# An audio tower on one core: the survival test of units A and B moved from VectorE to ScalarE, with new cyclic orders for all engines

## The reference

```python
def _ssm_layer(x, A_log, Dp, W_dbc, W_dt, b_dt):
    A = -jnp.exp(A_log)
    dbc = jnp.einsum('ble,ce->blc', x, W_dbc)
    delta, Bm, Cm = jnp.split(dbc, [DT_RANK, DT_RANK + N_STATE], axis=-1)
    delta = jax.nn.softplus(jnp.einsum('blr,er->ble', delta, W_dt) + b_dt)
    dA = jnp.exp(delta[..., None] * A)
    dBx = (delta * x)[..., None] * Bm[:, :, None, :]
    _, hs = jax.lax.associative_scan(combine, (dA, dBx), axis=1)
    return jnp.einsum('blen,bln->ble', hs, Cm) + Dp * x
...
h = _L0_tok_ref(x, ...)
h = h + _L0_attn_ref(_layernorm(h), ...)
h = h + _L0_ffn_ref(_layernorm(h), ...)
```

## Time and profile before

| | us |
|---|---|
| median of 3 runs (853.54 to 854.91) | 853.97 |
| the profiled execution, its own time | 855.28 |
| its span | 851.8 |
| PE busy (share of the span) | 708.0 (83%) |
| DVE busy | 644.6 (76%) |
| ACT busy | 531.3 (62%) |
| POOL busy | 342.4 (40%) |
| mean granted TensorE clock | 0.947 |

### The profile page before, as it was taken

The page is one execution under the profiler, slowest core; times in us unless marked ns, Lnnn a source line. Parts: engine busy times, 40 slices in busy tenths (PEclk is TensorE's granted clock), DMA queues, the critical chain, the costliest instruction groups (busy, mean ns, idle before and its releaser), DMA issues.

```text
span 851.8 us, 18852 instructions
## 1 busy us (share of the span) xinstructions
PE 708.0 (83%) x7751; PEld 320.4 (38%) x7751; DVE 644.6 (76%) x1075; ACT 531.3 (62%) x930; POOL 342.4 (40%) x291
## 2 busy tenths in 40 slices
PE   4736678898999989898989898989899879786863
PEld 2312233344444444343434444434444333332321
DVE  5746878889887888888988888888988886545231
ACT  1323365868686786868686868585868666553621
POOL 7225453536263535344443535352625351201000
PEclk9976899999999999999999999999999999879777
DMA  3221221202111120202030302020211010000000
GB/s 75 51 49 43 66 46 24 59 11 48 23 46 33 32 48 22 57 17 63 7 72 2 71 8 69 11 60 19 49 31 33 2 24 2 14 4 8 2 9 22
DMA packets 78562, 28.30 MB, mean 33 GB/s; under 512 B 70276, under 2 KB 78468, under 8 KB 78468
## 3 DMA queue, kind: packets, MB, share of 16 engines
q1 hardware_dynamic: 75268, 26.43, 13.6%
q10 hardware_dynamic: 3200, 0.58, 0.4%
HBM read 13.28 MB, written 3.05 MB: 19 GB/s over the span
## 4 chain that ended last, share of the span: by engine, by line
PE 53%; DVE 25%; ACT 7%; POOL 5%; issue 4%; SPq 3%; DMA 2%; POOLq 0%; DVEq 0%; ACTq 0%
PE ring L797 16%; PE ring L865 5%; PE ring L924 3%; PE ring L804 3%; PE ring L933 3%; PE ring L853 3%; DVE attT L1175 3%; PE ring L770 3%; DVE carry_A L1103 3%; PE ring L808 2%; PE ring L829 2%; DVE st L1212 2%; PE ring L915 2%; ACT hid L696 2%; SPq L379 2%
## 5 line engine op out<-in xcount | busy, mean ns | idle before, releaser
L661 ACT ACTIVATE pm<-ring,two_col 93x744 f32<-93x744 f32 x128 | 105.0, 872 | 22.2 <-PE ring L853 22.0
L517 POOL TENSOR_TENSOR h_in<-base_D,carry_D 128x372 f32<-128x372 f32 x16 | 15.7, 980 | 210.7 <-DVE h_mid L1180 204.6
L1225 DVE TENSOR_TENSOR hidw<-hid,ring 128x744 f32<-128x744 f32 x48 | 44.6, 929 | 49.0 <-PE ring L915 39.3
L853 PE MATMUL ring<-q_exp,qk 32*93 32x372 f32 x512 | 60.2, 540 | 8.6 <-POOL q_exp L535 6.5
L933 PE MATMUL ring<-nrm_f,w 64*64 64x372 f32 x384 | 43.5, 525 | 28.1 <-DVE quad_D L1095 21.7
L865 PE MATMUL ring<-pm,v 97*32 97x93 f32 x2048 | 57.3, 255 | 10.9 <-ACT pm L661 10.9
L696 ACT ACTIVATE hid<-ring,b_col 128x372 f32<-128x372 f32 x96 | 49.4, 567 | 23.3 <-PE ring L933 23.2
L597 ACT ACTIVATE soft_A<-ring,bdt_col 128x744 f32<-128x744 f32 x16 | 14.1, 881 | 78.9 <-PE ring L797 78.9
L535 POOL TENSOR_TENSOR q_exp<-qk,mask_q 128x1488 f32<-128x1488 f32 x16 | 42.9, 2683 | 44.5 <-DVE qk L1161 43.0
L513 POOL TENSOR_TENSOR du_C<-delta_C,x_C 128x744 f32<-128x744 f32 x16 | 29.1, 1817 | 76.2 <-ACT delta_C L609 76.2
L865 PEld LDWEIGHTS ring<-pm,v 97*32 97x32 f32 x2048 | 43.3, 114 | 38.4 <-ACT pm L661 22.4
(11 more groups left out here) (277 smaller groups left out, 1904.8 us busy)
## 6 DMA issues: line engine op xcount, KB each, us to landing
xin_A<-in_x_dram SPq DMA_DIRECT2D x62, 93.0 KB
xin_B<-in_x_dram SPq DMA_DIRECT2D x62, 93.0 KB
x_A<-x_A SPq DMA_DIRECT2D x32, 93.0 KB, 2.2
x_B<-x_B SPq DMA_DIRECT2D x32, 93.0 KB, 2.9
x_C<-x_C SPq DMA_DIRECT2D x32, 93.0 KB, 2.2
out_dram<-osb SPq DMA_DIRECT2D x16, 186.0 KB
x_D<-x_D SPq DMA_DIRECT2D x32, 46.5 KB, 1.9
w<-in_L_ffn_expert_w_dram SPq DMA_DIRECT2D x10, 48.0 KB
```

What stands on the lines that cost most here:

```text
L661: a.activation(pm[q % 2][h][0:TOUT].rearrange("m a j n -> m a (j n)"), out_of(f"att.s{q}{h}")[0:TOUT, :, 0:COLS], ACT.Square, bias=two_col ...
L853: ins = mm(o[h][0:TOUT, b, 0:COLS], qk[r:r + 32, 1, q * TOUT:(q + 1) * TOUT], q_exp[r:r + 32, q].rearrange("p j n -> p (j n)"), start=True ...
L1225: tt(hidw[k][:], hid2[:], out_of(f"ffn.g_{k}")[:, :, 0:COLS], ALU.mult).then_inc(me, 1)
```

## The change

For A and B the step `alive` goes from DVE to ACT. It was a minimum over delta (L1091). It becomes an activation Relu(delta * decay_max + 87.5) whose accumulator sums over the row: the sum is zero exactly if no element is above the bound. Its elementwise output goes to tile dec, which `decay` then overwrites, so it stands between `ln` and `decay` and waits for the `scan` of the group before. In C and D the minimum stays. The flags are read accordingly. Besides, all five cyclic orders and the bank table are new; the work in them is otherwise the same.

```diff
+        def alive(u):
+            return f"{'act' if u in 'AB' else 'dve'} {u}.alive"
...
                 if s == "ln":
                     need(g, f"act {u}.exp")
-                    need(g, f"pool {u}.du", f"act {u}.decay", *([f"dve {u}.alive"] if g < NG else []), back=1)
+                    need(g, f"pool {u}.du", f"act {u}.decay", *([alive(u)] if g < NG else []), back=1)
                     a.activation(delta[u][:] if g < NG else buf, buf, ACT.Ln, bias=1.0).then_inc(me, 1)
+                if s == "alive":
+                    need(0, f"dve prep.w{l}")
+                    need(g, f"act {u}.ln")
+                    need(g, f"dve {u}.scan", back=1)
+                    a.activation(columns(dec[u][:], u), columns(delta[u][:], u), ACT.Relu, bias=under_col[:],
+                                 scale=decay_max[:, l:l + 1], accum_out=seen[:, 0, FLAG[u], g:g + 1]).then_inc(me, 1)
                 if s == "decay":
                     need(0, f"dve prep.w{l}")
+                    if g < NG and alive(u)[:3] == "act":
+                        need(g, alive(u))
...
-                    need(g, *(("pool B.pooled",) if u == "C" else x_ready(u)))
+                    need(g, *x_ready(u))
...
                     for u, l in UNITS.items():
+                        if alive(u)[:3] == "act":
+                            ts(seen[:, 0, FLAG[u]], seen[:, 0, FLAG[u]], 0.0, None, ALU.is_le).then_inc(q, 1)
...
         ORDER = {
-            "dve": ("A.alive:0 ffn.hn:4 D.alive:3 att.rk:3 att.rq:3 C.alive:2 att.v1:3 ffn.route1:4 att.hat:3 "
+            "dve": ("ffn.hidw2:5 D.base:3 B.base:1 att.att1:4 att.att0:4 D.scan:3 D.based:3 ffn.fin:5 att.mid:4 "
...
-            "pool": ("att.qe:4 C.du:2 ffn.split:5 D.du:3 B.du:1 A.y:1 D.y:3 A.pooled:1 C.y:2 B.y:1 C.pooled:2 "
-                    "B.pooled:1 A.du:0"),
-            "sp": ("A.swap:1 D.swap:3 C.swap:2 A.load:0 B.swap:1 ffn.store:7 B.load:0"),
+            "pool": ("A.pooled:2 B.pooled:2 att.qe:4 C.du:2 ffn.split:5 D.du:3 B.du:1 A.y:1 D.y:3 A.du:0 C.y:2 "
+                    "C.pooled:2 B.y:1"),
+            "sp": ("D.swap:4 B.swap:2 C.swap:3 B.load:1 A.swap:1 ffn.store:7 A.load:0"),
```

More of the change, by code:

```diff
@@ L191, in audio_tower @@
         ORDER = {
[20 rows of a table removed]
[20 rows of a table added]
         }
         BANK = dict([
-            *((job, 0) for job in "A.c att.s10 A.xT att.s31 ffn.h1_2 ffn.h2_2 D.c ffn.o B.c B.dpre att.v att.vs att.s01 C.gen".split()),
-            *((job, 1) for job in "att.proj att.var".split()),
-            *((job, 2) for job in "att.s21 B.z att.s30 att.nrow att.nb0 A.dpre att.cen att.qk A.z ffn.h1_0 ffn.h2_0".split()),
-            *((job, 3) for job in "att.y3 ffn.oT".split()),
-            *((job, 4) for job in "D.z ffn.h1_1 C.b att.y1 D.b ffn.h2_1 ffn.g_1 D.s B.s C.c B.xT att.n2 C.dpre att.s00 att.y0 A.gen B.gen D.gen prep.w0".split()),
-            *((job, 5) for job in "ffn.gT ffn.lg prep.w1".split()),
-            *((job, 6) for job in "att.s20 att.s11 C.z ffn.g_0 att.y2 B.b ffn.g_2 att.nb1 C.s ffn.cen D.dpre A.b A.s prep.w2".split()),
-            *((job, 7) for job in "ffn.var ffn.rh prep.qkvp".split()),
+            *((job, 0) for job in "att.y0 A.c att.s11 att.s31 ffn.h1_2 ffn.h2_2 B.s att.proj A.dpre C.s B.xT B.dpre D.dpre A.s att.s00 B.gen D.gen".split()),
+            *((job, 1) for job in "att.v".split()),
+            *((job, 2) for job in "att.s21 att.s10 A.xT att.s30 ffn.g_1 ffn.g_2 att.nb1 C.c att.var att.qk ffn.h1_0 att.s01".split()),
+            *((job, 3) for job in "att.cen".split()),
+            *((job, 4) for job in "D.z ffn.h1_1 C.b att.y1 D.b ffn.h2_1 B.b D.s att.nb0 D.c B.c ffn.lg A.b C.dpre A.gen C.gen prep.w2".split()),
+            *((job, 5) for job in "ffn.gT ffn.rh prep.qkvp".split()),
+            *((job, 6) for job in "ffn.h2_0 att.s20 C.z B.z ffn.g_0 att.y2 att.nrow ffn.o ffn.cen att.n2 A.z att.vs prep.w0".split()),
+            *((job, 7) for job in "att.y3 ffn.oT ffn.var prep.w1".split()),
         ])
@@ L1024, in prepare @@
                     q = sem("flag_sum")
-                    need(g, *(f"act {u}.exp" for u in UNITS), *(f"dve {u}.alive" for u in UNITS))
+                    need(g, *(f"act {u}.exp" for u in UNITS), *(alive(u) for u in UNITS))
                     for u, l in UNITS.items():
-                        ts(seen[:, 0, FLAG[u]], seen[:, 0, FLAG[u]], decay_max[:, l:l + 1], UNDERFLOW, ALU.mult, ALU.is_le).then_inc(q, 1)
+                        if alive(u)[:3] == "act":
+                            ts(seen[:, 0, FLAG[u]], seen[:, 0, FLAG[u]], 0.0, None, ALU.is_le).then_inc(q, 1)
+                        else:
+                            ts(seen[:, 0, FLAG[u]], seen[:, 0, FLAG[u]], decay_max[:, l:l + 1], UNDERFLOW, ALU.mult, ALU.is_le).then_inc(q, 1)
                     dve.wait_ge(q, 4)
```

## The result

The changed kernel takes 867.79 us (median of 4 runs, 867.34 to 869.18), against 854.30 for the kernel before in the same comparison: a ratio of 1.0161, 95% interval 1.0144 to 1.0179. It is slower by 13.5 us. The prediction said slower by 6.0, 860 in a range of 843 to 868: sign and range held, the size did not.

A forecast was written before the change was run, and what follows sets the result against it. Bound: a ring of waits, period 44.63 us, no engine full, forecast 45.5. 11.5 periods x 0.9 = +10.4, ends -4.6: +5.8 on the profiled 855.28, 861.1; 1.3 less for the median, 859.8, given as 860, range 843 to 868.

The forecast's parts named there:

- The tests cost nothing by themselves: Moving A.alive and B.alive from DVE to ACT: costed at nothing, at most 2 us in all.
- the fill: Start, while the ring fills: PE's swap wait ends 2.5 earlier, the later C chain gives back 0.9; -1.6 us.
- The chain from A.s to h1_1: Serial chain per group through base_A, ffn.top held beside du_C, scan_A, based_A and quad_D: 9.3 us.
- The stretch from h1_1 to A.s: PE work per group in the new order, 35.15 plus waits of 1.1 for gT, qk and vs: 36.2 us.
- How far the hold reaches: ffn.top's ninth step beside POOL's du_C: held gives period 45.5; if it ran on, 0.6 shorter, 44.9.
- The period term of the sum: Steady stretch: 11.5 full periods, each 0.9 us longer than now, +10.4 us.
- The two ends: Fill, first period and last three groups together: -4.6 us, between -9 and 0.
- the first period: First distance between groups, without ffn steps, so neither ffn.top nor its hold: -1 us.
- the last groups: Last three groups, without A: quad_D wait 1.2 less each, 0.4 given back at D.c; -2 us in all.
- A: Rival: du_C's hold misses the chain to h1_1; period 43.9, 841 us; chance 0.17.
- B: Rival: hold short or h1_1-to-A.s stretch tighter; period 44.4 to 44.9, 847 to 853 us; chance 0.18.
- C: Rival: further waits at links taken as ready; period 46.4, 870 us; chance 0.13.

The follow-up runs named there:

- r2: Changed kernel with the tests of A and B back on DVE, behind C.based; 868.29 us, ratio 1.0150 to the kernel before.
- r1: Kernel before, its orders and banks kept, with the tests of A and B on ACT and A.decay behind att.rnorm; 863.14 us, ratio 1.0085.
- r10: Changed kernel with POOL's du_C multiplying only 12 of 372 columns per half from group 1 on; 848.99 us, single time.
- r3: Changed kernel with A.based moved behind D.quad and A.carry on DVE; 853.30 us, ratio 1.0010 to the kernel before.
- r7: r3 with A.based moved further, behind C.vin, and prep.late in front of A.quad of group 2; 854.62 us, ratio 1.0001.
- r9: r3 with A.based moved further, behind C.vin, and prep.late left in place; 853.23 us, ratio 0.9979.
- r14: Changed kernel run once more, unedited, with a second profile of its own; 865.04 us, single time.
- r6: Changed kernel with A.scan moved in front of A.base and ffn.top on DVE; 891.56 us, ratio 1.0425.
- r4: Changed kernel with DVE's prep.late moved from before D.quad of group 0 to before A.quad of group 2; 865.40 us, ratio 1.0105.
- r5: r3 with C's exp and ln later on ACT, behind hid2_0, and D.z behind s2 on PE; 869.06 us, ratio 1.0164.
- r8: r3 with the ninth step of ffn.top made a tensor_scalar with one SBUF input; 860.40 us, single time.

## Why the prediction came out as it did

- **The tests cost nothing by themselves**: right in the new order (r2). In the old order the move cost 8.5 us (r1), 2.7 of it in the fill with a collision that the text had not considered; it had costed the removal at nothing "by itself".
- **The chain from A.s to h1_1**: right. Forecast 9.3, measured 397.05 - 388.08 = 8.97. top started 1.73 after A.s (forecast 1.76), du_C 3.41 (3.57), its end 5.23 (5.38), and it met the ninth step. r10 shows that this hold was worth 1.16 of the period, r3 that based_A alone was worth 0.57.
- **The stretch from h1_1 to A.s**: 45.24 - 8.97 = 36.27, forecast 36.2. Of its waits gT was 0.52 (0.6), qk 0.22 (0.4) and vs none (0.1).
- **How far the hold reaches**: the held case was taken, and a plain tensor_tensor is held. A period of 44.9 did not come.
- **The period term of the sum**: mis-sized. 0.61 and not 0.9 per group makes 7.0 for 11.5 of them and not 10.4. In the first pair of profiles it counts 3.7, since the sum set 44.63 against every distance of an execution in which two were 46.29; 4.4 with the second pair.
- **The step that failed is "The two ends".** It had -1.6 for the fill, -1 for the first period and -2 for the last groups. The two pairs of profiles give +2.5, +0.8 and +2.4, so +5.7 where -4.6 stood (+8.7 in the first pair). In the fill I followed PE's wait for the swap, which did shrink by 2.3, and not what DVE runs next: eight small steps in front of D.quad moved beside three POOL instructions, the very mechanism that I had priced in the steady stretch. In the first period the same mechanism took other steps, but r10 shows that taking the larger of these holds away changes nothing; the cause of its +0.8 is open. For the last groups, the new orders run at 199.0 to 200.7 in six profiles (r2, r3, r7, r9, r10, r14), at 202.3 in r6 and at 204.7 to 206.9 in four (the changed kernel, r4, r5, r8), against 199.6 and 201.7 for the kernel before: the 2 us of gain are not there. (By its own terms the text had 3 x 0.8 = 2.4.) Why they are missing was not traced. How often an execution draws the longer end was not settled; the four executions of the changed kernel behind the median have a mean granted clock of 0.940 to 0.944 and 867.3 to 869.2 us, r14, with the shorter end, 0.951 and 865.04.
- **What is left open**: the medians differ by 13.5 and the spans of two profiles each by 10.0. Where the remaining 3.5 lies is not shown; between two profiles of one kernel the pieces that moved most are single distances and the end, where the granted clock differs.

The rivals: A and B (no hold on the chain, or a shorter one) did not happen. C (more waits) did not in the steady stretch. All of the excess over the forecast came from outside it. In the first pair of profiles the periods came out 6.7 under their term and the ends 13.3 over theirs. That the time fell inside the range, at its edge, owes something to these two errors having opposite signs.
